# Node scores of a graph attention layer by one-column products on TensorE, with turned blocks kept for the node rows

## The reference, cut to what matters

```python
h = relu(layernorm(x))                        # x: 6250 x 128
edge_h = concat([h[src], edge_attr], axis=1)  # 100000 edges
edge_m = edge_h @ a.T                         # a: 128 x 256 = [A1 | A2]
p      = exp(-leaky_relu(edge_m @ a_2[0], 0.2))
out    = x + segment_sum(p * edge_m, src) / segment_sum(p, src)
```

## Time and profile before

| | |
|---|---|
| median of three runs | 1156.25 us (1155.75 to 1156.82) |
| the profiled execution | 1157.21 us, its span 1155.5 us |
| GpSimd | 806.9 us busy, 70% |
| VectorE | 834.4 us busy, 72% |
| ScalarE | 622.5 us busy, 54% |
| TensorE | 611.8 us busy, 53% |
| moved by DMA | 291.55 MB, 252 GB/s in the mean |
| granted TensorE clock | 0.738 in the mean of the span |

### The profile page before, as it was taken

One profiled execution on the slowest core, in us unless ns is written; L12 is line 12 of the kernel. 1 busy time (PEld: TensorE's weight loads), 2 busy tenths in 40 slices (PEclk: granted clock), 3 DMA queues, 4 the chain that ended last, 5 costly groups with the idle time before them and its releaser, 6 DMA issues. The chain is left out here.

```text
span 1155.5 us, 21963 instructions
## 1 busy us (share of the span) xinstructions
PE 611.8 (53%) x5524; PEld 539.6 (47%) x5525; DVE 834.4 (72%) x3065; ACT 622.5 (54%) x2067; POOL 806.9 (70%) x826
## 2 busy tenths in 40 slices
PE   1144446246762163111655168762767562979997
PEld 0143436235551153111544167652656452778886
DVE  7986976888689957543557969768486543957787
ACT  3926435547562344423545257962376652888775
POOL 2727776777778777777777777777777777777402
PEclk9975758557786576555768578885578786989999
DMA  9999994999873744749887478974797769679744
GB/s 285 359 337 369 384 335 140 317 348 324 303 235 102 251 127 132 261 136 340 262 283 251 131 268 264 314 242 130 234 353 260 239 209 298 193 270 295 250 148 112
DMA packets 203971, 291.55 MB, mean 252 GB/s; under 512 B 19368, under 2 KB 144519, under 8 KB 203751
## 3 DMA queue, kind: packets, MB, share of 16 engines
q1 hardware_dynamic: 160852, 167.63, 45.4%
q10 hardware_dynamic: 18002, 69.95, 17.6%
q0 software_dynamic: 25024, 52.90, 12.9%
HBM read 158.94 MB, written 131.47 MB: 251 GB/s over the span
## 5 line engine op out<-in xcount | busy, mean ns | idle before, releaser
L563 POOL DMA_INDIRECT ordered_rows<-feed,dest x782 | 767.5, 982 | 267.3 <-issue 241.3
L885 PE MATMUL psum<-back,hots 128*128 128x129 f32 x2128 | 335.6, 316 | 36.1 <-DVE hots L1212 25.3
L885 PEld LDWEIGHTS psum<-back,hots 128*128 128x128 f32 x2128 | 300.0, 222 | 76.3 <-issue 74.9
L717 ACT ACTIVATE apart<-lanes,back 128x128 bf16<-128x128 bf16 x504 | 161.3, 389 | 184.9 <-PE psum L885 154.9
L660 ACT ACTIVATE feed<-feed 128x128 f32<-128x128 f32 (+1 forms) x784 | 238.7, 387 | 0.2 <-issue 0.2
L850 PE MATMUL psum<-score_parts,place_hot 128*128 128x50 bf16 x2352 | 99.6, 204 | 244.5 <-DVE place_hot L1116 224.9
L850 PEld LDWEIGHTS psum<-score_parts,place_hot 128*128 128x128 bf16 x2352 | 90.8, 110 | 255.5 <-DVE place_hot L1116 233.8
L1116 DVE TENSOR_SCALAR place_hot<-place_rows,lane 128x1024 bf16<-128x1024 bf16 (+1 forms) x98 | 52.0, 530 | 171.2 <-SPq L412 169.4
L1125 DVE SCALAR_TENSOR_TENSOR junk<-feed,psum 128x128 bf16<-128x128 f32 x784 | 169.8, 279 | 0.0
L652 ACT ACTIVATE feed<-leaky 128x8 f32<-128x8 f32 (+2 forms) x98 | 20.4, 208 | 245.0 <-DVE leaky L1148 245.0
L1212 DVE TENSOR_TENSOR hots<-psum,back 128x512 f32<-128x512 f32 (+1 forms) x133 | 94.4, 710 | 4.0 <-DMA back<-ordered_rows 4.0
(11 more groups left out here) (161 smaller groups left out, 734.1 us busy)
## 6 DMA issues: line engine op xcount, KB each, us to landing
ordered_rows<-empty SPq DMA_DIRECT2D x19, 3696.0 KB, 18.2
back<-ordered_rows ACTq DMA_DIRECT2D x123, 528.0 KB
feed<-in_edge_attr SPq DMA_DIRECT2D x97, 512.0 KB, 6.2
place_rows<-places SPq DMA_DIRECT2D x98, 256.0 KB, 5.8
ordered_rows<-feed,dest POOLq DMA_INDIRECT x782
back<-ordered_rows SPq DMA_DIRECT2D x10, 528.0 KB
self_part<-acc ACTq DMA_DIRECT2D x1, 3234.0 KB, 15.0
acc<-in_x SPq DMA_DIRECT2D x4, 768.0 KB, 8.5
```

The source lines that it names most:

```text
L563: pool.indirect_dma_start(out=ordered, out_offset=bass.IndirectOffsetOnAxis(ap=dest[:, n:n + 1], axis=0), in_=feed[:, n * ROW:(n + 1) * RO ...
L717: act.activation(apart[:, v * P:(v + 1) * P], lanes[:, :], ACT.Abs, bias=tags[:, u, PLACE:PLACE + 1], scale=-1.0).then_inc(apart_done, 1)
L885: last = pe.matmul(psum[:, bass.ds(outs[u], FEAT + 1)], hots[:, hot_buffer(k) * GT + u, :], back[:, n:n + FEAT + 1], start=False, stop=u = ...
```

## The change

`node_w` becomes one column, on the partitions the 128 features. GpSimd's seven products and ScalarE's 49 sums are gone. ScalarE's relu is interleaved with copies of turned units: behind the relu of unit n comes the copy of the turned unit n - 1 into `reluT`, which lies where `node_terms` lay and keeps all 49 turned windows. TensorE's new `node_unit(n)` turns the three windows of a unit as they come from the relu, then takes the products of the unit before with `node_w`, one column per window, into PSUM bank 4, from where VectorE reads the scores. Its units stand in TensorE's program at "stats" (0 to 7), behind `rank_sums` of chunk 0 (8 to 11) and among the first 25 picks of chunk 0 (12 to 16). "self" no longer turns anything: it is 49 products with `reluT` and 17 copies.

```diff
+UNITS_FIRST = 8
...
-        node_w = sb("node_w", [P, FEAT], F32)
+        node_w = sb("node_w", [P, 1], F32)
...
-        SCORES = 6
+        NODE_DOTS, SCORES = 4, 6
...
-        node_terms = back[:, 0:WINDOWS * FEAT].rearrange("p (w f) -> p w f", f=FEAT)
+        reluT = back[:, 0:WINDOWS * FEAT]
...
-            pool.wait_ge(weights_copied, 4)
-            for i in range(WINDOWS // RG):
-                at = slice(RG * i, RG * i + RG)
-                pool.wait_ge(relu_done, RG * (i + 1))
-                pool.tensor_tensor(node_terms[:, at, :], acc_w[:, at, 0:FEAT],
-                                   node_w[:, :].rearrange("p (a f) -> p a f", a=1).to_broadcast([P, RG, FEAT]),
-                                   ALU.mult).then_inc(terms_done, 1)
...
-                for w in range(WINDOWS):
-                    act.activation(acc[:, w * ROW:w * ROW + FEAT], acc[:, w * ROW:w * ROW + FEAT], ACT.Relu,
-                                   bias=moments[:, w, 0:1]).then_inc(relu_done, 1)
-                for w in range(WINDOWS):
-                    act.wait_ge(terms_done, w // RG + 1)
-                    act.activation(node_terms[:, w, :], node_terms[:, w, :], ACT.Copy, accum_out=score[:, w:w + 1]).then_inc(dots_done, 1)
+                def turned(n):
+
+                    at = windows_of(n)
+                    act.wait_ge(selfT_done, n + 1)
+                    act.copy(reluT[:, at.start * P:at.stop * P], bank(n % 2, 0, (at.stop - at.start) * P)).then_inc(selfT_copied, 1)
+
+                for n in range(FIN_UNITS):
+                    for w in range(WINDOWS)[windows_of(n)]:
+                        act.activation(acc[:, w * ROW:w * ROW + FEAT], acc[:, w * ROW:w * ROW + FEAT], ACT.Relu,
+                                       bias=moments[:, w, 0:1]).then_inc(relu_done, 1)
+                    if n > 0:
+                        turned(n - 1)
+                turned(FIN_UNITS - 1)
...
-                act.wait_ge(dots_done, WINDOWS)
+                act.wait_ge(dots_done, FIN_UNITS)
                 for n in range(FIN_UNITS):
...
+                    save(n)
                 act.wait_ge(self_copied, FIN_UNITS)
...
-            pe.matmul(bank(SCORES, 0, P), a2_wide, a_sb[:, 0:FEAT], start=True, stop=True)\
+            pe.matmul(bank(SCORES, 0, 1), a_sb[:, 0:FEAT], a2_wide[:, 0:1], start=True, stop=True)\
...
+            def node_unit(n):
+
+                def dots(n):
+
+                    pe.wait_ge(selfT_copied, n + 1)
+                    for w in range(WINDOWS)[windows_of(n)]:
+                        last = pe.matmul(bank(NODE_DOTS, w, 1), reluT[:, w * P:(w + 1) * P], node_w[:, :], start=True, stop=True)
+                    last.then_inc(dots_done, 1)
+
+                if n >= 2:
+                    pe.wait_ge(selfT_copied, n - 1)
+                for w in range(WINDOWS)[windows_of(n)]:
+                    pe.wait_ge(relu_done, w + 1)
+                    last = pe.transpose(bank(n % 2, (w - NW * n) * P, P), acc_w[:, w, 0:FEAT], ident[:, :])
+                last.then_inc(selfT_done, 1)
+                if n > 0:
+                    dots(n - 1)
+                if n == FIN_UNITS - 1:
+                    dots(n)
+
             def self_products():
...
+                pe.wait_ge(selfT_copied, FIN_UNITS)
+                for n in range(FIN_UNITS):
                     if n >= 2:
                         pe.wait_ge(self_copied, n - 1)
...
+                    for w in range(WINDOWS)[windows_of(n)]:
+                        last = pe.matmul(bank(2 + n % 2, (w - NW * n) * P, P), reluT[:, w * P:(w + 1) * P], A1w[:, :], start=True, stop=True)
                     last.then_inc(self_done, 1)
...
+                if what == "stats":
+                    pe.wait_ge(weights_copied, 4)
+                    for n in range(UNITS_FIRST):
+                        node_unit(n)
+                elif what == "scan":
                     rank_sums(at[0])
+                    if at[0] == 0:
+                        for n in range(UNITS_FIRST, 12):
+                            node_unit(n)
...
                         for i in range(BUCKETS // BB):
                             pick_sums(i)
+                            if 12 + i < FIN_UNITS:
+                                node_unit(12 + i)
...
-                dve.wait_ge(dots_done, WINDOWS)
+                dve.wait_ge(dots_done, FIN_UNITS)
...
-                done(dve.tensor_tensor(full, full, rstd[:, :], ALU.mult))
+                done(dve.tensor_tensor(full, bank(NODE_DOTS, 0, WINDOWS), rstd[:, :], ALU.mult))
```

More of the change, by code:

```diff
@@ L284, in gnn_kernel @@
             edge_dots place_hot_done window_hot_done chosen_done zed_done node_scores leaky_done prob_done tagged
-            dve_hot apart_done act_hot step_done rest_cleared first_cleared ranked relu_done terms_done dots_done selfT_done selfT_copied self_scaled pool_added rest_zero acc_done inv_done scaledT_done scaledT_copied
+            dve_hot apart_done act_hot step_done rest_cleared first_cleared ranked relu_done dots_done selfT_done selfT_copied self_scaled pool_added rest_zero acc_done inv_done scaledT_done scaledT_copied
             out_ready self_added result_done final_loaded kept_done stored""".split()
@@ L291, in gnn_kernel @@
          edge_dots, place_hot_done, window_hot_done, chosen_done, zed_done, node_scores, leaky_done, prob_done, tagged,
-         dve_hot, apart_done, act_hot, step_done, rest_cleared, first_cleared, ranked, relu_done, terms_done, dots_done, selfT_done, selfT_copied, self_scaled, pool_added, rest_zero, acc_done, inv_done, scaledT_done, scaledT_copied,
+         dve_hot, apart_done, act_hot, step_done, rest_cleared, first_cleared, ranked, relu_done, dots_done, selfT_done, selfT_copied, self_scaled, pool_added, rest_zero, acc_done, inv_done, scaledT_done, scaledT_copied,
          out_ready, self_added, result_done, final_loaded, kept_done, stored) = (sem(n) for n in names)
@@ L353, in scatters, with windows_of @@
             return GT * rounds - (GT - LAST_TILES if rounds == ROUNDS and k == RG - 1 else 0)
+        def windows_of(n):
+            return slice(NW * n, min(WINDOWS, NW * n + NW))
         def row_tags(slot):
@@ L603, in _ @@
             act.wait_ge(weights_step, 2)
-            act.copy(node_w[:, :], bank(SCORES, 0, P)).then_inc(weights_copied, 1)
+            act.copy(node_w[:, :], bank(SCORES, 0, 1)).then_inc(weights_copied, 1)
             act.wait_ge(pool_set, 25)
@@ L821, in table_sums @@
                           start=True, stop=True).then_inc(pairs_done, 1)
+            def node_unit(n):
[14 more added lines that the diff above has]
+                    dots(n)
             def self_products():
-                def product(n):
-                    pe.wait_ge(selfT_copied, n + 1)
+                pe.wait_ge(selfT_copied, FIN_UNITS)
+                for n in range(FIN_UNITS):
                     if n >= 2:
                         pe.wait_ge(self_copied, n - 1)
-                    for k in range(min(WINDOWS, NW * n + NW) - NW * n):
-                        last = pe.matmul(bank(2 + n % 2, k * P, P), last_T[:, n % 2, k, :], A1w[:, :], start=True, stop=True)
+                    for w in range(WINDOWS)[windows_of(n)]:
+                        last = pe.matmul(bank(2 + n % 2, (w - NW * n) * P, P), reluT[:, w * P:(w + 1) * P], A1w[:, :], start=True, stop=True)
                     last.then_inc(self_done, 1)
[L834 to L843, removed]
             def look_up(g):
@@ L897, in _ @@
                     look_up(groups[0])
-                if what == "scan":
+                if what == "stats":
[3 more added lines that the diff above has]
+                elif what == "scan":
                     rank_sums(at[0])
+                    if at[0] == 0:
+                        for n in range(UNITS_FIRST, 12):
+                            node_unit(n)
                 elif what == "rank":
```

2 lines of the change are left out of this document (removed).

## The result

The changed kernel takes 1165.03 us, the median of 6 runs (1162.14 to 1167.26), against 1156.53 us (1155.38 to 1158.54) for the kernel before beside it on the same chip: a ratio of 1.0073 [1.0056, 1.0091]. It is slower by 8.5 us. The prediction said 1156.3 us, 1151 to 1160, and gave 0.15 to any slowing; it was wrong. The profiled execution shown here took 1167.26 us, 10.05 more than that of before.

The account below looks back on a forecast made before the run. GpSimd's queue of scatters, between head and tail, was taken to bound the kernel. The head's -9.4 us would be lost at group 8, leaving +0.4 on 1156.25, less a little: 1156.3 us, range 1151 to 1160.

Parts of the forecast that it names:

- GpSimd's seven products go, six instructions fall, -10.1 us: Head, chunk 0: without GpSimd's products, six slowed VectorE instructions return to their medians, 10.1 us sooner.
- I take 0.9 us: Head, TensorE: assumed time added per three-window unit of transposes and one-column products; upper bounds 1.00 full clock, 1.92 half.
- the clock of the first 70 us is 1.00: Head, TensorE: the profile's clock column, 1.00 over the first 70 us, read as full clock for the new units.
- TensorE follows it: Head, node units: ScalarE needs 1.3 us a unit, so it sets the pace and TensorE keeps up.
- The picks' term: Head, chunk 0: five units among the first 25 picks, 0.4 us or so each, mostly given back: 0 to 1 us.
- the half-rate case: Head, TensorE at half clock: units up to 1.92 us, some 8 us more, head still 0 to 2 us shorter.
- rival E: Head as long as now; group 8's 7.61 us wait swallows that; forecast's time, chance 0.60 together with the forecast.
- groups 2 to 8 and on to group 11: After the head: transferred bytes set group 8's start, +0.4 us; the chain to group 11 is unchanged, GpSimd only waits longer.
- A: First scatter to group 8: the head's 9.4 us gain arrives whole, 1146.8 us; chance 0.07.
- B: Before group 8, or at the stretched scatter: part of the gain arrives, 2.5 to 6 us, 1152 us; chance 0.18.
- C: Around group 8: the self rows' write gets ahead of it, +4 us, 1160.5 us; chance 0.07.
- D: Later scatters: a shifted offset puts one more inside a VectorE comparison run, +5 us, 1161.3 us; chance 0.08.

Follow-up runs that it names:

- the removal alone: Kernel before without GpSimd's seven products and ScalarE's 49 sums, node-vector product left out, nothing new on TensorE: 1154.05 against 1153.75 us, 1.0000.
- wide products: Changed kernel with the node vector repeated in 128 columns, so each product is 128 wide, same scores: 1154.01 against 1153.75 us, 0.9992.
- The head made late: Kernel before with 40 more small copies on VectorE in "nodes", nothing else: 1166.53 against 1153.75 us, 1.0103.
- the move alone: Kernel before with VectorE's start of group 8 moved behind the scan of chunk 1, nothing else: 1151.05 us, 0.9986.
- both together: Changed kernel with 128-column products and VectorE's start of group 8 moved behind the count and scan of chunk 1: 1147.38 us, 0.9935.
- with work ahead: Changed kernel with 160 unused bf16 products on TensorE ahead of the node units: 1166.38 against 1153.75 us, 1.0093.

## Why the prediction was wrong, and where it was right

**Right: GpSimd's seven products go, six instructions fall, -10.1 us.** They did, in the change and in the removal alone: `shift` is done 10.2 us earlier. The Trainium skill, SBUF — State Buffer, § Who interferes with whom, has a VectorE instruction with two inputs in SBUF, or a fast copy or scalar operation, contend with a GpSimd instruction that reads SBUF; the six back at 0.19 to 0.48 us agree.

**Wrong: "I take 0.9 us", "the clock of the first 70 us is 1.00", "TensorE follows it".** The unit took 1.81 us; the upper bound of 1.92 that stood beside it was the value to take. At full rate 0.9 might have been close (a wide unit: 1.0); no run has a one-column unit at that rate. Every later number of the head hangs on this: first_tiles 5.41 us instead of 0 to 0.5, picks 9.9 us of waits instead of 0 to 1, first scatter 85.92 instead of 67.4. The picks' term was too small at full rate as well: with wide products they waited 3.7 us, and the first scatter came at 69.50, outside 66.7 to 68.2.

**Wrong: the half-rate case, "some 8 us more, and the head is 0 to 2 us shorter than now".** It had the right mechanism and less than half its size: from the forecast's head of -9.4 us to the measured +9.1 are 18.5 us, not 8. By its words it counted the excess of five and twelve units; it left out that a unit between picks costs its whole length once TensorE, not VectorE, paces the picks, and that the picks themselves slow down.

**Wrong: rival E, "group 8's wait of 7.61 us swallows that as well".** This joined the late case to the forecast's time, and made a slowing look improbable. The wait's other end is SyncE, which had itself been waiting 25.4 us for VectorE; that row was read for a head that comes early, and not for one that comes late. The head made late shows it: no part is swallowed. The prediction's own sign of being wrong came true: the first scatter and the one behind the hole moved by the same 9.1 us.

**Right: groups 2 to 8 and on to group 11.** Where the head was early (removal alone, wide products), group 8 started at 115.2 and 115.0, and the time did not move. Rivals A and B fall for those two kernels. No cost of the self rows is seen: in the wide kernel their write left at 122.57, behind group 8 (C did not happen). Of D, one scatter of 1.65 us is new, at 800.82; none of over 3 us is.

**Of the total,** 9.07 us are in place by 207 us. The profiled pair differs by 10.05, the medians by 8.5; the rest is within the spread of the runs, and nothing more is shown of it.

## What to carry to other kernels

A wait for a transfer covers a late engine only if the queue that orders the transfer does not wait for that same engine: look at the waits of the queue before counting on it, once for an early and once for a late arrival. Take TensorE's rate from the durations of known passes near the spot. And before an engine's idle time is used for added work, ask who stands behind that work in its program, at both rates; here the price was not the product but the picks queued behind it.

An early head is worth something only together with the next place that holds the work: wide products alone (0.9992) gave nothing that could be told from no change, the move alone at most the 4.5 us of the old hole (0.9986, or 0.997 without its one outlying run), both together 0.9935.

## What was not expected of the hardware

- **More columns made TensorE faster.** With one-column products in its units it was busy for 42 us at 1.2 GHz; with 128-column products in the same program it went to 2.4 GHz at about 32 us. The Trainium skill, TensorE: Matmul & The Clock Gate, Part 1, describes half rate as the default that activity of the array releases. The trace of the wide products agrees; the one-column kernel was not released, though TensorE was busy 40.31 of 41.00 us (with work ahead). A rate that other work had raised before the units did not last into them; a pause of 2.35 us lay between. Which part of a unit keeps the rate low wasn't tried separately: only the width was changed.
- **The clock column shows 1.00 from the start, whatever the rate, until the first change is on record.** Passes ran at half rate under it until about 58 us in the kernel before and 74 us in the change; where busy work ahead had put a change on record, the same units read 0.50 from 26 us on.
- **The stretched scatter of 6 us comes and goes.** At its place it is 6.01 us in the profiles of before, of the change, of the change with busy work ahead and of the wide products with the move behind the scan; 4.84 and 3.69 us in two others, 1.41 us in the removal alone and with wide products alone, and missing in two. The removal alone has another of 5.36 us at 626.27. That is of the size of the spread between runs of one kernel; that it makes the spread was not shown.
